# P V of an attention layer in five blocks instead of eight: values of the second key chunk beside them, fewer and wider copies

## The reference

```python
x = x + attention(layernorm(x))      # 16 heads of 64, rope, 4 memory keys ahead of 256, causal softmax
x = x + ffn(layernorm(x))            # a gated scan over the 32 batches, then tanh(x wo + c uo + bo)

h = rms_norm(x); q, k, v = split(h @ w_qkv.T)
scores = rope(q) @ concat(pm_k, rope(k)).T * scale
out = softmax(causal(scores)) @ concat(pm_v, v)      # "P V"
out = out @ w_out.T
c = sigmoid(x_t wf + c uf) * c + sigmoid(x_t wi + c ui) * tanh(x_t wc + c uc)
```

## Time and profile before

| | us |
|---|---|
| median of 3 runs | 1124.64 (1124.19 to 1130.9) |
| profiled execution, its own time | 1127.17 |
| span of the profiled execution | 1125.4 |
| PE busy | 1079.8 (96%) |
| DVE busy | 934.1 (83%) |
| ACT busy | 698.1 (62%) |
| POOL busy | 633.8 (56%) |

### The profile page before, as it was taken

How to read it: one execution, slowest core, us unless ns; L and a number is a source line. 1 busy time by engine, 2 the same in 40 slices (tenths; PEclk the granted TensorE clock), 3 DMA queues, 4 the chain that set the end, 5 groups by cost and what they waited for, 6 DMA issues and landing times.

```text
span 1125.4 us, 47265 instructions
## 1 busy us (share of the span) xinstructions
PE 1079.8 (96%) x18443; PEld 814.4 (72%) x18443; DVE 934.1 (83%) x3306; ACT 698.1 (62%) x1575; POOL 633.8 (56%) x819
## 2 busy tenths in 40 slices
PE   4979999999999999999999999999999999999996
PEld 2557777777777777777777777777777777777775
DVE  6778888888888888888888888888887889888645
ACT  3746665666666666666666666566675666666634
POOL 4546565556656555665565576565566566656510
PEclk8989999999999999999999999999999999999998
DMA  6222433432333333233333333333332333333215
GB/s 208 105 85 88 115 112 110 120 115 86 95 112 115 116 115 116 78 103 111 116 116 115 108 96 92 111 112 111 115 98 87 113 109 110 111 111 103 71 23 150
DMA packets 78031, 120.52 MB, mean 107 GB/s; under 512 B 13041, under 2 KB 35954, under 8 KB 77682
## 3 DMA queue, kind: packets, MB, share of 16 engines
q1 hardware_dynamic: 68714, 111.20, 32.4%
q10 hardware_dynamic: 9096, 6.30, 2.2%
HBM read 41.56 MB, written 8.78 MB: 45 GB/s over the span
## 4 chain that ended last, share of the span: by engine, by line
PE 66%; DVE 14%; DMA 10%; SPq 3%; issue 3%; POOL 1%; ACT 1%; DVEq 0%; POOLq 0%; ACTq 0%
PE bank_pv L1173 12%; PE bank L1065 12%; PE bank_st L1129 9%; DMA rope_c<-rope_b 7%; PE bank_sum L1210 6%; PE bank_sum L1194 5%; PE bank_sm L1104 4%; DVE masked L835 4%; PE bank L1087 4%; DMA linv_scratch<-linv 3%; PE bank L1084 2%; PE bank L1312 2%; PE bank L1314 2%; PE bank_st L1133 2%; SPq L312 2%
## 5 line engine op out<-in xcount | busy, mean ns | idle before, releaser
L419 POOL TENSOR_TENSOR qk<-rope_a,rope_c 128x512 f32<-128x512 f32 x256 | 341.0, 1332 | 301.2 <-DMA rope_c<-rope_b 293.4
L835 DVE CUSTOM_DVE_ANT_0 masked<-bank_sm,mask_q 128x132 bf16<-128x132 f32 (+1 forms) x1024 | 307.1, 354 | 16.5 <-PE bank_sm L1104 15.7
L412 POOL TENSOR_TENSOR prob<-prob 128x264 f32<-128x264 f32 x256 | 209.5, 818 | 120.0 <-ACT prob L559 113.4
L824 DVE TENSOR_TENSOR rope_a<-bank,cos 128x512 f32<-128x512 f32 x256 | 174.0, 680 | 121.5 <-PE bank L1065 80.7
L544 ACT ACTIVATE qk_h<-qk 128x512 f16<-128x512 f32 x256 | 160.4, 626 | 167.9 <-POOL qk L419 167.2
L559 ACT ACTIVATE prob<-bank_st 128x784 f32<-128x784 f32 x256 | 209.0, 817 | 60.3 <-PE bank_st L1138 59.6
L1173 PE MATMUL bank_pv<-prob,v_sb 128*64 128x256 f32 (+1 forms) x2048 | 224.7, 340 | 0.8 <-DVE raw L851 0.6
L1129 PE MATMUL bank_st<-qk 64*64 64x256 f32 (+3 forms) x4096 | 186.2, 299 | 0.2
L1129 PEld LDWEIGHTS bank_st<-qk 64*64 64x64 f32 x4096 | 167.7, 134 | 9.2 <-issue 0.9
L825 DVE TENSOR_TENSOR rope_b<-bank,sin 128x512 f32<-128x512 f32 x256 | 173.7, 679 | 0.0
L1173 PEld LDWEIGHTS bank_pv<-prob,v_sb 128*64 128x64 f32 x2048 | 124.3, 136 | 54.6 <-issue 1.3
(11 more groups left out here) (241 smaller groups left out, 1738.1 us busy)
## 6 DMA issues: line engine op xcount, KB each, us to landing
rope_c<-rope_b SPq DMA_DIRECT2D x512, 128.0 KB, 2.4
rinv<-linv_scratch SPq DMA_DIRECT2D x124, 256.0 KB, 4.7
out<-x_sb SPq DMA_DIRECT2D x16, 256.0 KB, 3.7
linv_scratch<-linv SPq DMA_DIRECT2D x62, 64.0 KB, 2.0
x_sb<-x ACTq DMA_DIRECT2D x28, 128.0 KB, 5.4
xt<-w_qkv_t ACTq DMA_DIRECT2D x1, 1024.0 KB, 5.4
v_end<-v_end_scratch SPq DMA_DIRECT2D x64, 8.0 KB
v_sb<-pm_v SPq DMA_DIRECT2D x63, 8.0 KB
```

What stands on the lines that cost most here:

```text
L412: G.tensor_tensor(prob_2[:, s % 4, :, :], prob[:, s % 4, :, 0:NT - Q1], prob[:, s % 4, :, C0 + Q1:SCOL], ALU.add).then_inc(S["prob_added"], 1)
L419: G.tensor_tensor(qk[:, s, :].rearrange("p (u n) -> p u n", u=2)[:, :, 0:NT], rope_a[:, (NPAIR * j + s) % 3, :].rearrange("p (u n) -> p u ...
L824: V.tensor_tensor(rope_a[:, (NPAIR * j + s) % 3, :], proj_bank(j, s)[:, :], cos[:, :], ALU.mult)
L835: ins = V.tensor_tensor_reduce(masked[:, e, c0:c0 + n], ps_sm[:, e, c0:c0 + n], mask_q[:, c0:c0 + n], 1.0, LOWEST, ALU.add, ALU.max, top[: ...
```

## The change

`attend` of the eight pairs no longer runs once in every step, but in five blocks: pair 7 in step 0, pairs 0 and 1 in step 2, 2 and 3 in step 4, 4 in step 5, 5 and 6 in step 7. The second pair of a block goes to the other half of `bank_pv`, and `raw_copy` takes both halves in one instruction. The values of the second key chunk (blocks 3 and 1, L1087) move behind the scores of their step, directly ahead of P V; their copies move behind the exponential of the step.

```diff
+PV_AT = {0: (7,), 2: (0, 1), 4: (2, 3), 5: (4,), 7: (5, 6)}
...
-            def raw_copy(bj, par, s):
-                act.wait_ge(S["pv_ready"], NPAIR * bj + s + 1)
+            def raw_copy(bj, par, pairs_of):
+                s, n = pairs_of[0], len(pairs_of)
+                act.wait_ge(S["pv_ready"], NPAIR * bj + s + n)
...
-                A.activation(raw[:, par, s, :], ps_pv[:, 0:NT], ACT.Copy, scale=1.0 / RS).then_inc(S["raw_done"], 1)
+                A.activation(raw[:, par, s:s + n, :].rearrange("p s q -> p (s q)"), ps_pv[:, 0:n * NT], ACT.Copy,
+                             scale=1.0 / RS).then_inc(S["raw_done"], n)
...
-                    if s in (3, 4) and b:
-                        value_copy(j - 1, s - 1)
+                    if s == 3 and b:
+                        value_copy(j - 1, 2)
...
-                    if s == 7 and a:
+                    if s == 7 and a and j == 0:
                         value_copy(j, 1)
...
                     if b:
                         exp(j - 1, s)
+                    if s == 4 and b:
+                        value_copy(j - 1, 3)
+                    if s == 7 and a and j > 0:
+                        value_copy(j, 1)
...
-                    if s >= 1 and b:
-                        raw_copy(j - 1, 1 - p, s - 1)
+                    if s in (2, 4, 5, 7) and b:
+                        raw_copy(j - 1, 1 - p, PV_AT[s])
...
-            def attend(bj, s):
+            def attend(bj, s, at):
...
-                wait(pe, S["raw_done"], NPAIR * bj + s)
+                if at == 0:
+                    wait(pe, S["raw_done"], NPAIR * bj + s)
...
-                        last = T.matmul(ps_pv[OWN[e], q0:NT], v_sb[:, kc, col:col + DH], prob[:, s % 4, e, c0:c0 + NT - q0],
+                        last = T.matmul(ps_pv[OWN[e], at + q0:at + NT], v_sb[:, kc, col:col + DH], prob[:, s % 4, e, c0:c0 + NT - q0],
...
-                    if s in (3, 4) and b:
-                        values(j - 1, 1 - p, s - 1)
+                    if s == 3 and b:
+                        values(j - 1, 1 - p, 2)
...
-                    if s == 7 and a:
+                    if s == 7 and a and j == 0:
                         values(j, p, 1)
...
                     if b:
                         scores_t(j - 1, s)
...
-                    if s >= 1 and b:
-                        attend(j - 1, s - 1)
+                    if s == 4 and b:
+                        values(j - 1, 1 - p, 3)
+                    if s == 7 and a and j > 0:
+                        values(j, p, 1)
+                    if s in (2, 4, 5, 7) and b:
+                        for i, pair in enumerate(PV_AT[s]):
+                            attend(j - 1, pair, i * NT)
```

More of the change, by code:

```diff
@@ L684, in body @@
                         exp(j - 1, s)
+                    if s == 4 and b:
+                        value_copy(j - 1, 3)
+                    if s == 7 and a and j > 0:
+                        value_copy(j, 1)
                     if s == 0 and c:
-                        raw_copy(j - 2, p, NPAIR - 1)
+                        raw_copy(j - 2, p, PV_AT[0])
                     if s == 0 and j == NB + 1:
@@ L1386, in body @@
                     if s == 0 and c:
-                        attend(j - 2, NPAIR - 1)
-                    if s >= 1 and b:
-                        attend(j - 1, s - 1)
+                        attend(j - 2, NPAIR - 1, 0)
+                    if s == 4 and b:
[5 more added lines that the diff above has]
+                            attend(j - 1, pair, i * NT)
                     if s == 0 and c:
```

## The result

| | before | changed |
|---|---|---|
| median, us | 1127.66 (1124.19 to 1130.9, 4 runs) | 1156.56 (1154.27 to 1158.21, 4 runs) |
| span of the profiled execution | 1125.4 | 1152.5 |
| ratio to before, 95% interval | | 1.0255 [1.021, 1.0301] |

The changed kernel is 28.9 us slower. 1155 was forecast, 1140 to 1167 was the range.

What follows compares the result with a forecast made beforehand. PE and VectorE were taken as chains of equal length, only work in stretches PE sets counting. +0.71 - 0.11 + 0.40 = +1.00 us a turn, times 30, on the 1124.64 median gave 1154.6, rounded to 1155; range 1140 to 1167.

Steps and rivals of the forecast that it cites:

- steps 1 and 2: Pair 0 moves to step 2; turned maxima of step 3 still wait for VectorE: 0, bounds 0 and -0.1.
- steps 3 and 4: Savings of 0.21 against a 0.23 wait of step 4's scores for VectorE's maxima: 0.02, taken as 0.
- border of 6 and 7: Pair 5 behind step 7's turned maxima costs +0.71 us a turn, PE idle ahead; L1087 beside P V -0.11.
- wait for the copy: Step 7's scores wait for ScalarE's copy of turned maxima: 0.5 in 20 turns, 0.2 in 10, +0.40 average.
- steps 5 and 6: Stretch ahead of step 7's turned maxima; the prediction's sum had no term of its own for it.
- third rival: The copy's wait in step 7 doesn't come, the rest does: 0.60 a turn, 18 us, 1143 us; chance 0.15.
- fourth rival: ScalarE late in step 7; L1227 or next scores wait 0.5 a turn, another 15 us: 1170; chance 0.08.
- covered at nothing: Fewer P V copies on ScalarE, later value copy in step 7: no cost, cover before step 0's L1227 about 0.9.
- Filling and draining: Turn 1 (filling) and turn 32 (draining): both within 2 us, taken at 0.
- signs that were named: Changed profile: PE idle 25 us before step 7's turned maxima; step 7's scores wait for the copy 10 us or more.

Runs made afterwards that it cites:

- e3: The changed kernel with the f32 scores (scores_t) ahead of the f16 scores for the maxima in step 7; 1146.44 us, ratio 1.0163.
- e2: The changed kernel with pair 5 back in step 6 and step 7's second-chunk values and their copy in their old places; 1129.2 us, ratio 1.002.
- e4: e3 with the projection ahead of the turned maxima in step 7; 1131.58 us, ratio 1.0048.
- e1: The changed kernel with P V of pair 5 back in step 6, so six blocks; 1142.75 us, ratio 1.0128.
- e7: Kernel before, eight P V blocks, second-chunk values beside P V in steps 4 and 7, copies later, f32 scores first in step 7; 1136.19 us.
- e8: The changed kernel with pair 5 back in step 6, f32 scores first in step 7, VectorE's inversion ahead of pair 6's maxima; 1135.55 us.
- e9: e7 with ScalarE's second norm behind the exponential and the value copy in step 7; 1129.15 us, ratio 1.0013.
- e10: e9 with VectorE's inversion ahead of the maxima of pair 6 in step 1; 1107.43 us, ratio 0.982.
- e11: Kernel before with only the second norm moved behind the exponential in step 7; 1126.45 us, ratio 0.9986.

## Why the prediction was right, and where its sizes were off

The mechanism held. The sum was 1.00 us a turn where 0.85 was measured, mostly because one term was twice too large.

| term, us a turn | predicted | measured |
|---|---|---|
| steps 1 and 2 | 0 | 0 (7.96 both times, means of the two steps) |
| steps 3 and 4 | 0.02 | -0.01 (7.31 against 7.32) |
| border of 6 and 7, less L1087 | 0.71 - 0.11 | 0.52 to 0.54 |
| wait for the copy | 0.40 | 0.21 |
| steps 5 and 6 | 0 | 0.11 |
| sum | 1.00 | 0.85 |

The last three measured rows come from cutting each turn at its turned maxima, on the mean over the 28 turns. From `invert` to those of step 3 are 4.08 in every kernel that has `invert` in its old place. From there to those of step 7 are 17.42 before and 17.53 with the change. From those of step 7 to `invert` are 11.45 before, 12.19 with the change and 11.98 in e3, in which the copy's wait is covered.

**Steps 1 to 4** gave nothing, as said. The turned maxima of step 3 stand 4.08 behind the inversion in both kernels with 0.19 of idle PE on record instead of 0.04, and e2 shows it by itself. At the scores of step 4 the record has 0.17 of idle time for the predicted 0.23. It counts from the recorded end of the last matmul, which lies some 0.07 behind the next possible start, so that the two agree.

**The border** is the loss. In e3 the way from the turned maxima of step 7 to `invert` is 11.96 in nearly all turns, against 11.44 or (VectorE late) 11.42 before: 0.52 to 0.54, where 0.71 less 0.11 was forecast. Most of the difference is the pair's own price. P V of step 7 up to the sums, before and then changed:

```profile
264.22 0.88 PE L1173 MATMUL bank_pv<-prob,v_sb 128*64 128x256 f32 x8
265.03 0.65 PE L1194 MATMUL bank_sum<-prob,ones_sum 128*32 128x124 f32 x16
```

```profile
674.69 1.48 PE L1181 MATMUL bank_pv<-prob,v_sb 128*64 128x256 f32 x16
676.10 0.64 PE L1202 MATMUL bank_sum<-prob,ones_sum 128*32 128x124 f32 x16
```

The step pays 1.41 instead of 0.81, 0.60 more for the second pair and not 0.71, and ahead of the turned maxima nothing was saved. In e4 other work in that hole brings back half of the loss. The Trainium skill's page TensorE: Matmul & The Clock Gate, section The mechanism, says that matmuls start strictly in program order; the 0.73 at 671.70, with the projection standing behind it that e4 then runs in this very time, agrees.

**The wait for the copy** was mis-sized, by half: 0.21 a turn, some 6 us, against 12. This is the term that takes most from the sum. Two things were wrong in it. In an undisturbed turn the scores start 1.30 behind the turned maxima instead of the 0.87 that PE needs: 0.43, not 0.51, since ScalarE's cast starts 0.03 behind the turned maxima (671.73), where I had it 0.12 behind (261.94 less 0.28, against 261.54). And undisturbed turns are fewer than I counted. Of turns 2 to 31 ten have the full idle time of 0.36 on record and five have 0.20 to 0.30; in the other fifteen VectorE was later still. Those look like this, PE and then ScalarE:

```profile
502.35 0.29 PE L1119 MATMUL bank_sm<-ident_b,top 128*128 128x128 bf16 x2 [1.35 <-DVE top L842]
...
503.32 0.34 PE L1111 MATMUL bank_sm<-qk_h 64*64 64x68 f16 x8
```

```profile
502.67 0.51 ACT L575 ACTIVATE top_t<-bank_sm 128x128 bf16<-128x128 f32 x3 [0.18 <-PE bank_sm L1119]
```

Here too the scores follow the copy's end (503.18) by 0.14, but only 0.10 later than PE could start them, for the predicted 0.18. The 0.41 between L1112 and the copy in the earlier trace rows was misread: ScalarE was not free there, it went through `raw_copy`, cast and end keys without a pause from 621.49 to the copy. With no `raw_copy` ahead it is 0.32. The third rival (no wait there) would have been 1143 and had 0.15; e3, which removes it, measured 1146.

**Steps 5 and 6** were taken at nothing. The 0.11 there is the share of late turns, which the sum doesn't have. It is 0.02 in e3 and 0.00 in e1 against before, so no part of the change can be made answerable for it.

**The fourth rival** (ScalarE late) did not cost the changed kernel anything, but it was real: e7 and e8 ran into it as soon as step 7 was short again. The price of "covered at nothing" depended on a microsecond that the change itself added.

**Filling and draining** were taken at 0 with a bound of 2; 27.1 - 23.7 leaves 3.4, of which 1.7 are the two other turns of the 30. That the total came so near is in part luck. Thirty turns of 0.85 are 25.4 us, not 30, and the rest up to 28.9 comes from the ends and from the spread of the medians. And the forecast added its 30 to a median of 1124.64, where all runs together give 1127.66: 1.1 too much and 3.0 too little leave 1155 only 1.6 below the measured 1156.56.

Of the signs that were named all but one showed: PE idle before the turned maxima of step 7 (0.73 for 0.8; of the 42.8 us some 7 are at the head of step 3 and 5.2 in filling, which leaves 31 for 25), the scores of step 4 released by the maxima, 4.08 unchanged, 12.35 for 12.4, PE's share from 96% to 92%. The scores of step 7 were released by the copy for 5.6 us, not for 10 or more.

## What to carry to other kernels

- An engine that is 96% busy can still be waiting at every meeting point: ask at each whether what stands ahead of the wait is filling it. In this kernel work in front of a wait was free as long as it fitted in, the same work behind it cost its full length, and a saving in front of a wait was worth nothing.
- Look first at the engine that is waited for. Swapping two calls on VectorE gave 11 us where savings of 0.1 us per change of tile form on the busy engine gave none; with that slack in hand two of these savings became worth 8 us.
- A timeline of one undisturbed turn priced terms to about 0.1 us here, but says nothing about how many turns are late. Count those in every variant: e9 gained 0.29 in the undisturbed turn and nothing in the time.

## What the runs showed of the hardware

- L1087 directly ahead of P V made step 4 shorter by 0.15 us and step 7 by 0.12 (e7, e9, e10), a little more than the 0.10 that the rows of before gave for one change of form.
- Two P V pairs in one block behind L1087 took 1.41 us (674.69 to 676.10 in the changed kernel), one pair there 0.76 (e1), one pair between other forms 0.81 (before).
- PE started 0.14 to 0.15 us behind the end of ScalarE's copies (672.85 to 673.00, 799.50 to 799.64). Behind the end of VectorE's last maxima it was 0.15 as well at `scores_for_max` (34 waits in the changed kernel), but 0.06 at the turned maxima (all 61 waits). So the shorter distance belongs to those matmuls and not to VectorE; why stays open.
- GpSimd's small operations for the norm, not the exponentials, made ScalarE stand: 7.4 us in all before, 48.3 after, and what decides it is the value copy ahead of it: 38.9 in e1, 7.3 in e2, where that copy is back in its place. With the norm behind the exponential it is 1.1 (e9, e10, e11).
